# A graph-masked attention layer on one core: V made one step behind the scores, Q and K products in one go, and another order of loads and stores

## The reference

```python
q = heads(x @ Wq + bq); k = heads(x @ Wk + bk); v = heads(x @ Wv + bv)
scores = einsum('bhqd,bhkd->bhqk', q, k) / sqrt(64)
bias = where(adj, 0.0, -9e15)[:, None]
probs = softmax(scores + bias, axis=-1)
ctx = einsum('bhqk,bhkd->bhqd', probs, v)        # heads side by side again: 384
y = x + ctx @ Wf + bf
out = (y - mean(y)) / sqrt(var(y) + 1e-5)
```

## Time and profile before

| What | Value |
|---|---|
| median of 3 runs | 1043.46 us (1042.8 to 1044.99) |
| the profiled execution: its own time, its span | 1043.48 us, 1041.7 us |
| PE busy | 1018.5 us, 98% of the span |
| PEld busy | 907.3 us, 87% |
| DVE busy | 733.8 us, 70% |
| POOL busy | 631.1 us, 61% |
| ACT busy | 593.2 us, 57% |
| share of PE in the chain that ended last | 96% |
| mean granted TensorE clock | 0.993 |

### The profile page before, as it was taken

How to read it: one execution, slowest core, us unless ns; L and a number is a source line. 1 busy time by engine, 2 the same in 40 slices (tenths; PEclk the granted TensorE clock), 3 DMA queues, 4 the chain that set the end, 5 groups by cost and what they waited for, 6 DMA issues and landing times.

```text
span 1041.7 us, 26751 instructions
## 1 busy us (share of the span) xinstructions
PE 1018.5 (98%) x7161; PEld 907.3 (87%) x7161; DVE 733.8 (70%) x2823; ACT 593.2 (57%) x2119; POOL 631.1 (61%) x652
## 2 busy tenths in 40 slices
PE   8999999999999999999999999999999999999975
PEld 7889889889888888889889889889888888888864
DVE  3576777777777777677677677677677677677564
ACT  3565655655655655655656656656656656656550
POOL 1356666666656656656656656656666665665675
PEclk9999999999999999999999999999999999999988
DMA  7266566666666666666666666666666666665443
GB/s 199 64 157 174 172 179 175 182 177 177 179 183 173 180 181 173 180 184 173 179 183 171 180 184 176 179 181 180 178 179 177 178 177 179 183 184 184 144 145 114
DMA packets 338970, 179.63 MB, mean 172 GB/s; under 512 B 222592, under 2 KB 322560, under 8 KB 338944
## 3 DMA queue, kind: packets, MB, share of 16 engines
q1 hardware_dynamic: 338544, 178.74, 62.0%
q10 hardware_dynamic: 400, 0.59, 0.2%
HBM read 103.75 MB, written 75.50 MB: 172 GB/s over the span
## 4 chain that ended last, share of the span: by engine, by line
PE 96%; DVE 2%; POOL 1%; DMA 1%; issue 1%; ACT 0%; SPq 0%; DVEq 0%; POOLq 0%
PE qk_ps L338 14%; PE cov_ps L338 13%; PE cov_ps L340 13%; PE cov_ps L339 13%; PE qk_ps L340 13%; PE qk_ps L339 13%; PE scores_ps L354 9%; PE cov_ps L368 8%; DMA x_in<-in_x 1%; DVE s_mask L500 0%; DVE stats L538 0%; DVE y_sb L532 0%; DVE wv_lo L468 0%; DVE p_turned L512 0%; POOL x_bias L702 0%
## 5 line engine op out<-in xcount | busy, mean ns | idle before, releaser
L628 ACT ACTIVATE probs<-s_mask,neg_max 128x128 f32<-128x128 f32 x768 | 297.5, 391 | 6.9 <-DVE neg_max L506 6.9
L500 DVE CUSTOM_DVE_ANT_0 s_mask<-scores_ps,mask_bias 128x128 f32<-128x128 f32 x768 | 172.5, 287 | 95.7 <-PE scores_ps L354 91.2
L719 POOL TENSOR_TENSOR probs<-probs,inv_sum 128x768 f32<-128x768 f32 x128 | 188.7, 1474 | 80.0 <-DVE inv_sum L519 80.0
L714 POOL TENSOR_SCALAR y_sb<-y_sb,mean_var,rstd 128x384 f32<-128x384 f32 x127 | 209.8, 1652 | 23.4 <-POOL rstd L708 23.4
L512 DVE STREAM_TRANSPOSE p_turned<-probs 128x768 f32<-128x768 f32 x128 | 125.2, 978 | 116.0 <-POOL probs L719 116.0
L708 POOL TENSOR_TENSOR rstd<-var_eps,minus_half 128x1 f32<-128x1 f32 x128 | 71.9, 562 | 179.3 <-DVE var_eps L544 179.3
L646 ACT ACTIVATE qT<-qk_ps,bq_col 128x512 f32<-128x512 f32 x96 | 65.5, 683 | 154.3 <-PE qk_ps L340 154.3
L628 ACT ACTIVATION_READ_ACCUMULATOR probs<-s_mask,neg_max 128x1 f32 x768 | 145.1, 189 | 0.0
L338 PE MATMUL cov_ps<-wf_hi,cT_hi 128*128 128x384 f32 x384 | 131.0, 341 | 11.6 <-DVE cT_lo L474 11.6
L621 ACT CAST cT_hi<-cov_ps 128x384 fp32r<-128x384 f32 x128 | 61.5, 480 | 137.7 <-PE cov_ps L368 134.9
L489 DVE TENSOR_TENSOR xT_lo<-xT,xT_hi 128x384 fp32r<-128x384 f32 x120 | 112.9, 979 | 33.1 <-ACT xT_hi L615 32.9
(11 more groups left out here) (57 smaller groups left out, 1974.6 us busy)
## 6 DMA issues: line engine op xcount, KB each, us to landing
p_out<-p_turned SPq DMA_DIRECT2D x128, 384.0 KB, 2.9
pT<-p_out SPq DMA_DIRECT2D x512, 96.0 KB, 2.2
x_in<-in_x SPq DMA_DIRECT2D x128, 192.0 KB, 2.6
out<-y_sb SPq DMA_DIRECT2D x128, 192.0 KB, 2.1
x_blocks<-in_x SPq DMA_DIRECT2D x360, 64.0 KB, 2.2
adj_u<-in_adj SPq DMA_DIRECT2D x32, 64.0 KB, 2.1
y_sb<-in_L_gnn_Wq ACTq DMA_DIRECT2D x1, 576.0 KB, 4.7
s_mask<-in_L_gnn_Wk SPq DMA_DIRECT2D x1, 576.0 KB, 6.6
```

The lines of the kernel that those rows point to most:

```text
L500: last = nc.vector.tensor_tensor_reduce(out=s_mask[:, e, h, :], in0=scores_ps[:, score_cols(e, h)], in1=mask_bias[:, e, :], scale=SCALE, s ...
L628: last = nc.scalar.activation(probs[:, e, h, :], s_mask[:, e, h, :], ACT.Exp, bias=neg_max[:, e, h:h + 1], scale=1.0, accum_out=row_sum[:, ...
L714: nc.gpsimd.tensor_scalar(y_sb[:, y, :], y_sb[:, y, :], mean_var[:, e, 0:1], rstd[:, e, 0:1], ALU.subtract, ALU.mult).then_inc(y_ready, 1)
L719: nc.gpsimd.tensor_tensor(probs[:, e, :, :], probs[:, e, :, :], inv_sum[:, e, :].unsqueeze(2).broadcast_to([P, HEADS, SEQ]), ALU.mult).the ...
```

## The change

Seven edits, all in the order of work and in its buffers. The sum of the computation stays the same.

1. PE makes V one step *behind* the scores instead of two ahead: `v_product` in step p is for step p-1 (`V_LAG = 1`), and directly follows the output product, on the same PSUM bank. `copy_v` on ACT follows. The context product waits for its own V.
2. The three Q or K jobs of a step stand together, ahead of the output product.
3. The high and low parts of x are kept for four groups instead of two (`XT_RING = 4`), since V reads them later.
4. A pass of the hardware loop has 8 steps instead of 4; the indices in it are rewritten.
5. DVE: the residual sum of sample 0 stands behind the inverse sum of sample 1 and ahead of `p_turned` of sample 1, the residual sum of sample 1 behind that; `xT_lo` comes later, and both samples' statistics last.
6. SP: `x_in` and the mask are loaded first in a step; the store of `p_turned` of sample 0 stands ahead of `x_blocks`.
7. Start: the bias row's product uses a `cov_ps` bank, the first scores no longer wait for the bias row (the first V does), and the low part of Wv is made behind that of Wf.

The constants and the buffers:

```diff
-TURN = 4
+TURN = 8
...
+V_LAG = 1
...
+XT_RING = 4
...
+TURN_GROUPS = TURN * 2 // GROUP
...
-        xT_hi = sb("xT_hi", [P, 2, KC, GTOK], F32R)
+        xT_hi = sb("xT_hi", [P, XT_RING, KC, GTOK], F32R)
```

SP, in `step`:

```diff
+                if real(p + X_LEAD, PAIRS) and not by_matmul(2 * (p + X_LEAD)):
+                    for e in range(2):
+                        load_x(2 * (p + X_LEAD) + e, (2 * (c + X_LEAD) + e) % X_RING)
+                if c % 2 == 0 and real(p + 2, PAIRS):
+                    g, slot = TURN_GROUPS * i + c // 2 + 1, (c // 2 + 1) % 2
+                    sp.dma_start(adj_u8[:, slot, :, :],
+                                 adj[bass.ds(g * GROUP, GROUP), :, :].rearrange("b q k -> q b k")
+                                 ).then_inc(adj_loaded[slot], DMA)
                 if real(p - 1, PAIRS):
                     load_blocks(i, c - 1, 1, 2 * (p - 1) + 1)
...
-                if c % 2 == 0 and real(p + 2, PAIRS):
-                    g, slot = 2 * i + c // 2 + 1, (c // 2 + 1) % 2
-                    past(sp, masked_ready, 2 * (p - 1) + 1)
-                    sp.dma_start(adj_u8[:, slot, :, :],
-                                 adj[bass.ds(g * GROUP, GROUP), :, :].rearrange("b q k -> q b k")
-                                 ).then_inc(adj_loaded[slot], DMA)
+                if real(p, PAIRS):
+                    store_blocks(c, 0, 2 * p)
                 if real(p + BLOCKS_AHEAD, PAIRS) and not by_matmul(2 * (p + BLOCKS_AHEAD - c % 2)):
                     load_x_blocks(i, c, c % 2)
-                if real(p + X_LEAD, PAIRS) and not by_matmul(2 * (p + X_LEAD)):
-                    for e in range(2):
-                        load_x(2 * (p + X_LEAD) + e, (2 * (c + X_LEAD) + e) % X_RING)
                 if real(p, PAIRS):
-                    store_blocks(c, 0, 2 * p)
                     load_blocks(i, c, 0, 2 * p)
                     store_blocks(c, 1, 2 * p + 1)
```

PE, in `scores`, `ctx_product`, `v_product` and `step`:

```diff
-                        pe.wait_ge(bias_row_ready, 1)
...
-                if isinstance(p, int) and p - 1 + AHEAD >= PAIRS:
-                    past(pe, y_added, n - 2)
-                else:
-                    past(pe, v_copied, 2 * (p - 1 + AHEAD) + e)
+                past(pe, v_copied, n)
...
             def v_product(c, p, e):
-                n, at = 2 * (p + AHEAD) + e, 2 * (c + AHEAD) + e
-                par, tok = at // GROUP % 2, tokens(at)
+                n, at = 2 * (p - V_LAG) + e, 2 * (c - V_LAG) + e
+                par, tok = at // GROUP % XT_RING, tokens(at)
                 if isinstance(n, int) and n == 0:
                     past(pe, w_split["v"], KC - 1)
                 past(pe, xT_split, n)
                 if real(p - LAG, PAIRS):
                     past(pe, y_added, 2 * (p - LAG) + e)
-                else:
-                    past(pe, v_copied, n - 2)
+                elif e == 0:
+                    pe.wait_ge(bias_row_ready, 1)
...
-                for j in jobs[:2]:
+                for j in jobs:
                     qk_product(i, c, j)
...
                         out_product(c, p, e)
-                for j in jobs[2:]:
-                    qk_product(i, c, j)
-                if real(p + AHEAD, PAIRS):
+                if real(p - V_LAG, PAIRS):
                     for e in range(2):
                         v_product(c, p, e)
```

DVE, in `step`:

```diff
                     invert_sums(1, 2 * p + 1)
+                if real(p - LAG, PAIRS):
+                    add_residual(i, c, 0, 2 * (p - LAG))
+                if real(p, PAIRS):
+                    turn_blocks(i, c, 1, 2 * p + 1)
+                if real(p - LAG, PAIRS):
+                    add_residual(i, c, 1, 2 * (p - LAG) + 1)
                 if real(p + X_AHEAD, PAIRS):
                     for e in range(2):
                         split_x(c, e, 2 * (p + X_AHEAD) + e)
-                if early and p == -2:
-                    split_weight("v")
                 if early and p == -1:
                     dve.wait_ge(bias_mm, 1)
-                    nc.vector.tensor_tensor(bias_row[:, :], xT_bank(0)[:, 0:HID], bf_row[:, :], ALU.add
+                    nc.vector.tensor_tensor(bias_row[:, :], cov_ps[0][:, 0:HID], bf_row[:, :], ALU.add
                                             ).then_inc(bias_row_ready, 1)
                     split_weight("f")
-                if real(p - LAG, PAIRS):
-                    for e in range(2):
-                        add_residual(i, c, e, 2 * (p - LAG) + e)
-                    find_stats(c, 0, 2 * (p - LAG))
-                if real(p, PAIRS):
-                    turn_blocks(i, c, 1, 2 * p + 1)
-                if real(p - LAG, PAIRS):
-                    find_stats(c, 1, 2 * (p - LAG) + 1)
+                    split_weight("v")
+                if real(p - LAG, PAIRS):
+                    for e in range(2):
+                        find_stats(c, e, 2 * (p - LAG) + e)
```

More of the change, by code:

```diff
@@ L104, in attention_block @@
         xT = sb("xT", [P, 2, KC, SEQ])
-        xT_hi = sb("xT_hi", [P, 2, KC, GTOK], F32R)
-        xT_lo = sb("xT_lo", [P, 2, KC, GTOK], F32R)
+        xT_hi = sb("xT_hi", [P, XT_RING, KC, GTOK], F32R)
+        xT_lo = sb("xT_lo", [P, XT_RING, KC, GTOK], F32R)
         w_hi = {m: sb(f"w{m}_hi", [P, KC, HID], F32R) for m in "qkvf"}
@@ L254, in load_x_blocks @@
             def load_x_blocks(i, c, half):
-                g = 2 * i + (c + BLOCKS_AHEAD) // 2
+                g = TURN_GROUPS * i + (c + BLOCKS_AHEAD) // 2
                 slot = (c + BLOCKS_AHEAD) // 2 % 2
@@ L345, in scores @@
                 if e == 0:
-                    past(pe, qk_copied, 2 * i + c // 2, per=NJ)
+                    past(pe, qk_copied, TURN_GROUPS * i + c // 2, per=NJ)
                     if isinstance(n, int) and n == 0:
                         past(pe, xT_split, BY_MATMUL - 1)
-                        pe.wait_ge(bias_row_ready, 1)
                 past(pe, max_found, n - 2)
@@ L359, in ctx_product @@
                 n, at = 2 * (p - LAG) + e, 2 * (c - LAG) + e
-                past(pe, pT_landed[at % PT_RING], 2 * i + at // PT_RING, per=BLOCKS * DMA)
-                if isinstance(p, int) and p - 1 + AHEAD >= PAIRS:
-                    past(pe, y_added, n - 2)
-                else:
-                    past(pe, v_copied, 2 * (p - 1 + AHEAD) + e)
+                past(pe, pT_landed[at % PT_RING], 2 * TURN // PT_RING * i + at // PT_RING, per=BLOCKS * DMA)
+                past(pe, v_copied, n)
                 dst = cov_ps[e]
@@ L422, in bias_product @@
                 pe.wait_ge(bv_widened, 1)
-                past(pe, xT_split, GROUP)
                 for k in range(KC):
-                    last = nc.tensor.matmul(xT_bank(0)[:, 0:HID], bv_wide[:, k, :], w_raw["f"][:, k, :],
+                    last = nc.tensor.matmul(cov_ps[0][:, 0:HID], bv_wide[:, k, :], w_raw["f"][:, k, :],
                                             start=k == 0, stop=k == KC - 1)
@@ L479, in turn_x @@
                 par, b = at // GROUP % 2, at % GROUP
-                past(dve, x_blocks_loaded[par], i + (at - BY_MATMUL) // (2 * GROUP), per=KC * BLOCKS * DMA)
+                past(dve, x_blocks_loaded[par], TURN_GROUPS // 2 * i + (at - BY_MATMUL) // (2 * GROUP), per=KC * BLOCKS * DMA)
                 past(dve, xT_split, n - 2)
@@ L530, in add_residual @@
                 else:
-                    dve.wait_ge(y_stored[y], (2 * i + at // Y_RING) * DMA)
+                    dve.wait_ge(y_stored[y], (2 * TURN // Y_RING * i + at // Y_RING) * DMA)
                 nc.vector.tensor_tensor(y_sb[:, y, :], cov_ps[e][:, 0:HID], x_bias[:, at % X_RING, :], ALU.add
@@ L612, in round_x @@
                     past(act, x_turned, n - BY_MATMUL)
-                past(act, qk_done, 2 * i + at // GROUP - 2, per=NJ)
-                past(act, v_done, n - 2 * GROUP)
+                past(act, qk_done, TURN_GROUPS * i + at // GROUP - XT_RING, per=NJ)
+                past(act, v_done, n - XT_RING * GROUP)
                 nc.scalar.copy(xT_hi[:, par, :, tok], xT_source(n, e)).then_inc(xT_hi_ready, 1)
@@ L633, in copy_v @@
             def copy_v(c, e, n):
-                slot = (2 * (c + AHEAD) + e) % V_RING
+                slot = (2 * (c - V_LAG) + e) % V_RING
                 past(act, v_done, n)
@@ L668, in step @@
                     copy_qk(i, c, j)
-                if real(p + AHEAD, PAIRS):
+                if real(p - V_LAG, PAIRS):
                     for e in range(2):
-                        copy_v(c, e, 2 * (p + AHEAD) + e)
+                        copy_v(c, e, 2 * (p - V_LAG) + e)
             run_steps(act, step, PAIRS + LAG)
@@ L691, in make_mask_bias @@
                 par = at // GROUP % 2
-                past(pool, adj_loaded[par], i + at // (2 * GROUP), per=DMA)
+                past(pool, adj_loaded[par], TURN_GROUPS // 2 * i + at // (2 * GROUP), per=DMA)
                 past(pool, max_found, n - 2)
@@ L699, in add_bias @@
                 slot = (2 * c + e) % X_RING
-                past(pool, x_loaded[slot], i, per=DMA)
```

(1 more changed line is left out.)

4 lines of the change are left out of this document (2 added, 2 removed).

## The result

The changed kernel took 1055.86 us (median of 5 runs, 1052.96 to 1057.11); the kernel before took 1044.99 in its five. Ratio 1.0101, 95% interval 1.0084 to 1.0117. The profiled execution of after took 1054.52 with a span of 1052.7, 11.0 above that of before. The forecast was 1043.9, the range 1038.5 to 1054.0.

The account below looks back on a forecast made before the run. PE was taken as the bound, busy throughout the full steps, so only the ends could shrink. -4.3 + 0 + 6.3 + 0.1 - 1.7 = +0.4 on a span of 1041.7 gave 1043.9 us with the 1.8 around it; range 1038.5 to 1054.

Parts of the forecast that it names:

- Full steps, "0, between 0 and +0.25 a step": Sixty full steps: the new order costs 0, at most +0.25 us a step (15).
- the third: Rival: the longer loop is fetched again at each of six passes, 2.2 us each, at most 13; chance 0.15, slower.
- can only stay as they are or grow: Sixty full steps of 15.67 us: no matmul is removed or added, so they cannot get shorter.
- Start, "-4.3": Start, up to the scores of step 2: -6.0 us, or -4.3 with one expected clock fall.
- the 1.7 us set apart: Start: work lost to one expected fall of PE's clock to 1.2 GHz behind a wait.
- "+6.3": Step 62: V of sample 1 waits for the second residual sum, so the step grows from 8.14 to 14.45 us.
- "+0.1": Step 63, from scores to the next context: 14.0 us taken against 13.94 before.
- "-1.7": From the context after step 63 to the end: earlier output, no half-clock stretch, V added; between 0 and -3 us.
- Rival 2: Full steps: POOL's second normalise holds `neg_max`; 7 us in every other step (1051), 15 in every one (1059); chance 0.2, slower.
- SyncE, "zero, between 0 and 2.2": SyncE's queue moves: no cost, or at most one landing of 2.2 us, once.
- Rule weighed: Loop branch: a taken branch outside the buffered window fetches before going on, making a loop of twice the length worse.

Follow-up runs that it names:

- Runs 1 to 3: Changed kernel: 1, no loop, 1037.71 us; 2, three loop passes instead of six, 1043.81; 3, written out for PE alone 1059.37, all but PE 1050.7, PE and VectorE 1040.32.
- before_sp_jobs: Kernel before, four-step loop, with SyncE's new order and the three Q or K products in one go: 1043.54 us, ratio 1.0006.
- turn8_sp: Kernel before with eight steps in a loop pass and SyncE's new order: 1081.18 us, ratio 1.0365.
- after_flat: Changed kernel with no loop, every engine's 64 steps written out: 1037.71 us, ratio 0.9953 against the kernel before.
- after_flat_spold: Changed kernel written out, with SyncE's transfers in the order of the kernel before: 1061.66 us, ratio 1.0166 against the kernel before.
- run 5: Changed kernel written out with SyncE's old order: 1061.66 us; kernel before with its four-step loop and SyncE's new order alone: 1042.53 us.
- run 4: Kernel before written out without its loop: 1060.68 us; the same with SyncE's new order: 1042.76 us.

## Why the prediction was wrong

**Full steps, "0, between 0 and +0.25 a step".** This is the term that failed, and twice. The sum had nothing for the longer loop. The size at the jumps was 16.6 us; it stood among the rivals as the third with a chance of 0.15 and a price of up to 13, and the range took in only half of that. At its full price it gives 1056.5, and that this lies 0.6 from the measured 1055.86 is in part luck: it counts six refetches of 2.2 where there were five jumps of 3.3, and leaves out gains of 3.5 in the steps and 1.5 at the start. The argument against it was "with half of them nothing shows", but that the four-step loop is never refetched says nothing of one twice as long. Runs 1 to 3 show that the jumps back cost, and on which engines; that code is fetched there is read from the packets. The price from the nearest row, a landing of 2.2 us, was too low: VectorE's refetch kept it 4.2 to 5.2 us, and the clock fell behind two of five. I also looked at the instructions of PE alone; VectorE's loop was the dearer one.
Second, "can only stay as they are or grow" was wrong: with one change between products of 512 and of 384 columns less a step is 0.04 us shorter in before_sp_jobs, and 0.06 with VectorE's order as well. A PE that is never idle can still lose time between its instructions.

**Start, "-4.3".** It was -5.8, the -6.0 of the working. PE's idle stretches were 2.20 and 1.44 (said 2.4 and 3.4), and a clock fall came (0.69 from 33.8 to 37.0), but in steps that wait for other engines, so the 1.7 us set apart for it were not paid.

**End, "+6.3", "+0.1", "-1.7".** +5.7, -0.3, -1.7. V waited for `y_sb` as said.

**Rival 2, `neg_max` held.** It did not happen. DVE and POOL in a full step of after:

```profile
507.17 1.02 DVE L486 TENSOR_TENSOR xT_lo<-xT,xT_hi 128x384 fp32r<-128x384 f32 x2
...
512.23 0.17 DVE L503 TENSOR_SCALAR neg_max<-row_max 128x6 f32<-128x6 f32 x1
```

```profile
512.35 1.66 POOL L711 TENSOR_SCALAR y_sb<-y_sb,mean_var,rstd 128x384 f32<-128x384 f32 x1 [0.18 <-POOL rstd L705]
```

`xT_lo` takes the 1.0 us predicted. The second normalise starts at 2.65 into the step (scores at 509.70), as worked out; `neg_max` is there 0.12 us earlier. The runs also show that the price, a hold of 1.7 us, was wrong. In after_flat one `neg_max` started at 177.80, behind a normalise that had started at 177.74, and took its usual 0.17. In after_flat_spold 42 of them started 0.6 to 1.15 us into a normalise of 1.65 and took 0.17 each; 12 that started 1.15 to 1.5 us into it took 0.19 to 0.52 and ended with it. So such a meeting cost 0.35 us at the most. (Times on POOL are rough, and which engine reached the memory first they do not say.)

**SyncE, "zero, between 0 and 2.2".** Right in the loop of before (run 5), but as a reason it missed the point: the new order is the one part of the change that keeps the fetches of a kernel with code to fetch from costing 17 to 24 us more.

**Rule weighed.** The Trainium skill, page "Runtime: NRT & Kernel Launch", section "Instruction fetch mechanics", says that a taken branch to a target outside the buffered window fetches before it goes on. It adds that this is "one reason runtime control flow is expensive and why kernels prefer full unrolling where possible". Runs 1, 2 and 3 agree: 16.6 us at five jumps, none where the code is written out. By run 4 unrolling is no gain by itself: with SyncE's old order it cost 17 us.

## What to carry to other kernels

Before a loop body grows, look whether the instruction queues fall silent while it runs; if they do, the loop is resident and a longer one has to be tested against being written out. Price a jump by the engine that resumes last, with the clock behind it. And give the queue that issues the transfers slack. Its waits for a landing are none (293 us of them in the kernel before), as nothing behind them can be issued meanwhile; slack is when it waits for the engine whose result it stores. In a queue without slack delays add up and come out as another engine's wait.

## What the runs showed of the hardware that I had not expected

- A jump back to the head of the eight-step loop kept PE 2.0 to 2.5 us and VectorE 4.2 to 5.2 us; straight code with 58 q8 packets held neither of them up (after_flat: 60 full steps of 15.61).
- PE's granted clock was 0.65 and 0.63 over some 4.7 us behind idles of 2.20 and 2.25 us, but 1.00 behind 2.23 and 2.51 in the same trace; behind 4.9 us in two pieces (turn8_sp) it was 0.50 over 5.8 us.
- In SyncE's queue in the order of before, written out, longer issues (3.83 and 4.44 us for six instead of 3.07) added up over the steps until VectorE waited 3.3 us for a store.
- VectorE's `neg_max` was not held when it started in the first 1.15 us of POOL's normalise, and was held to its end, 0.35 us at most, when it started later.
